# Writes of padding rows spread between the row loads of an expert layer

## What is computed

```python
x = _layernorm(x + attention(x))
scores = softmax(xf @ gate_w.T)                    # 4096 tokens, 8 experts
top_vals, top_idx = top_k(scores, 2)
h = einsum('td,ehd->teh', xf, W1)                  # only for the chosen experts
y, g = split(h, 2); eo = einsum('teh,edh->ted', y * silu(g), W2)
z = einsum('te,ted->td', w_dense, eo)
z = z + _gated_mlp(xf, Ws1, Ws2)                   # the shared expert, all tokens
x = _layernorm(x + z)
```

## Time and profile before

| | |
|---|---|
| median of 3 runs | 350.71 us (349.76 to 352.3) |
| the profiled execution | 349.76 us |
| its span | 348.0 us |
| TensorE busy | 313.3 us, 90% of the span |
| VectorE busy | 265.5 us, 76% |
| GpSimd busy | 195.8 us, 56% |
| ScalarE busy | 192.8 us, 55% |
| mean granted TensorE clock | 0.966 |

### The profile page before, as it was taken

How to read it: one execution, slowest core, us unless ns; L and a number is a source line. 1 busy time by engine, 2 the same in 40 slices (tenths; PEclk the granted TensorE clock), 3 DMA queues, 4 the chain that set the end, 5 groups by cost and what they waited for, 6 DMA issues and landing times.

```text
span 348.0 us, 7780 instructions
## 1 busy us (share of the span) xinstructions
PE 313.3 (90%) x2225; PEld 281.1 (81%) x2225; DVE 265.5 (76%) x1037; ACT 192.8 (55%) x425; POOL 195.8 (56%) x223
## 2 busy tenths in 40 slices
PE   2889899999999989999998999999999999999800
PEld 1456688689788878888898999999999999999700
DVE  1796679766889898975577776676668998988786
ACT  1053787545565454635234566655565558868863
POOL 4049641746687858785372444444757685677620
PEclk9989999899999999999999999999999999999955
DMA  7968320311381202262145344444899798899668
GB/s 218 382 232 273 121 63 0 110 35 63 107 206 50 94 33 94 82 189 78 65 168 148 120 129 132 131 129 126 183 252 196 191 242 194 209 238 261 186 211 337
DMA packets 31383, 54.63 MB, mean 157 GB/s; under 512 B 4880, under 2 KB 22544, under 8 KB 31344
## 3 DMA queue, kind: packets, MB, share of 16 engines
q1 hardware_dynamic: 23136, 29.82, 28.8%
q0 software_dynamic: 8208, 24.32, 24.8%
HBM read 29.73 MB, written 24.40 MB: 156 GB/s over the span
## 4 chain that ended last, share of the span: by engine, by line
PE 63%; DVE 14%; DMA 8%; POOL 6%; ACT 4%; issue 3%; SPq 2%; POOLq 0%; DVEq 0%; ACTq 0%
PE bank L1061 21%; PE bank L945 12%; PE bank L1087 11%; PE bank L1070 5%; PE bank L1030 4%; PE bank L967 4%; DMA stage<-ws_t 4%; PE bank L930 3%; DVE xs L1173 3%; DVE htlo L1378 2%; POOL rows_in L559 2%; DVE mix L1373 2%; POOL w1lo L515 2%; DMA rows_out<-stage,place 1%; DMA stage<-w_t 1%
## 5 line engine op out<-in xcount | busy, mean ns | idle before, releaser
L599 POOL DMA_INDIRECT rows_out<-stage,place x71 | 69.2, 974 | 60.5 <-ACT stage L768 45.0
L559 POOL DMA_INDIRECT rows_in<-x,slot x64 | 65.2, 1019 | 50.2 <-DVE slot L1288 33.6
L1061 PE MATMUL bank<-w1hi,xthi 128*128 x142 | 39.2, 357 | 1.1 <-DVE xs L1384 1.1
L748 ACT ACTIVATE stage<-bank 128x384 f32<-128x384 f32 (+1 forms) x36 | 17.5, 487 | 40.5 <-PE bank L1061 40.5
L768 ACT ACTIVATE stage<-bank,weight 128x256 f32<-128x256 f32 x71 | 30.0, 471 | 15.5 <-PE bank L1087 15.4
L1061 PE MATMUL bank<-w1lo,xthi 128*128 x142 | 36.2, 336 | 0.0
L1061 PE MATMUL bank<-w1hi,xtlo 128*128 x142 | 36.2, 335 | 0.0
L686 ACT ACTIVATE mix<-bank 128x512 f32<-128x512 f32 x24 | 14.2, 592 | 36.3 <-PE bank L945 36.3
L1390 DVE TENSOR_TENSOR xtlo<-bank,xthi 128x512 fp32r<-128x512 f32 (+1 forms) x36 | 24.3, 676 | 11.1 <-ACT xthi L694 10.8
L1518 DVE TENSOR_TENSOR stage<-bank,stage 128x384 f32<-128x384 f32 (+1 forms) x36 | 19.8, 550 | 15.7 <-ACT stage L748 15.5
L945 PE MATMUL bank<-xthi,ws1hi 128*128 128x512 f32 x96 | 31.8, 412 | 0.0
(11 more groups left out here) (242 smaller groups left out, 895.6 us busy)
## 6 DMA issues: line engine op xcount, KB each, us to landing
stage<-rows_in SPq DMA_DIRECT2D x71, 133.0 KB, 2.9
xs<-rows_out POOLq DMA_DIRECT2D x12, 512.0 KB, 6.7
xs<-x SPq DMA_DIRECT2D x8, 512.0 KB, 8.7
out<-xs SPq DMA_DIRECT2D x7, 512.0 KB, 5.1
stage<-w_t SPq DMA_DIRECT2D x8, 384.0 KB, 3.9
rows_in<-clear SPq DMA_DIRECT2D x16, 133.0 KB
rows_out<-stage,place POOLq DMA_INDIRECT x71, 3.5
stage<-w_t SPq DMA_DIRECT2D x2, 512.0 KB, 3.9
```

What stands on the lines that cost most here:

```text
L559: pool.indirect_dma_start(rows_in[0:E * CAP, :], bass.IndirectOffsetOnAxis(slot[:, q * G + t, k:k + 1], 0), x2[q % 2][:, t, :], None).then ...
L599: pool.indirect_dma_start(rows_out[:, :], bass.IndirectOffsetOnAxis(place[:, 2 * j + b:2 * j + b + 1], 0), by[j % 4][:, b * C:(b + 1) * C] ...
L748: act.activation(bsg[j % 2][:, 0:width(j)], bank_h[j % 2][:, 0:width(j), H:F], ACT.Silu).then_inc(s_bsg, 1)
L1061: mm = pe.matmul(bank_h[j % 2][:, b, 0:F], bx[j % 2][:, (2 * b + k) * P:(2 * b + k + 1) * P], w[:, bass.ds(e, 1), k, :], start=(a == 0), s ...
```

## The change

Before, SyncE issues all 8 writes of padding in a row and then loads pairs 4 to 7. Now it loads pair 4, then issues 2 writes, loads pair 5, issues 2 writes, and so on to pair 7. The wait for `zrow` stays in front of pair 4. What is transferred, and all waits, are the same; only SyncE's program is reordered.

```diff
             for j in range(4):
                 load_rows(j)
             sp.wait_ge(s_ends, 1)
-            for e in range(E):
-                r = sp.value_load(zrow[0:1, e:e + 1], min_val=0, max_val=ROWS - P)
-                sp.dma_start(rows_in[bass.ds(r, P), :], clear[:]).then_inc(s_pad, 16)
+            share_of = E // (FULL // 2 - 4)
             for j in range(4, FULL // 2):
                 load_rows(j)
+                for e in range((j - 4) * share_of, (j - 3) * share_of):
+                    r = sp.value_load(zrow[0:1, e:e + 1], min_val=0, max_val=ROWS - P)
+                    sp.dma_start(rows_in[bass.ds(r, P), :], clear[:]).then_inc(s_pad, 16)
             for n in range(2):
                 sp.wait_ge(s_sc[n], 16 * K * G * NP)
             sp.wait_ge(s_pad, 16 * (IDLE + E))
```

## The result

| | median | range | runs |
|---|---|---|---|
| before | 351.07 us | 349.17 to 353.08 | 20 |
| changed | 354.1 us | 350.81 to 356.33 | 20 |

The ratio is 1.0072, with a 95% interval of 1.0049 to 1.0093: the changed kernel is slower, by about 2.5 us, or 3.0 us by the medians. I had forecast no change and a range up to 353.0. So the loss is under 1%, but it is real, and the median lies outside the range.

What follows compares the result with a forecast made beforehand. TensorE was taken to bound the kernel, busy 313.3 of 348.0 us. Pair 4, pairs 5 to 7, pair 8 and contention each added 0, so 349.76 us stayed, 350.7 as a median; range 349.2 to 353.0.

Steps and rivals of the forecast that it cites:

- The transposes of pair 5 began at 199.86: TensorE's transposes (L1030): pair 5's start read as 199.86 us, pairs 6 and 7 following in rounds of 4.12 us.
- the transposes of pair 8, which began at 212.22: TensorE's start on pair 8's rows, read as 212.22 us; the latest time by which pair 8's loads must land.
- The rival on the hand-over: Change-over to expert blocks: without writes beside last scatters or first loads, experts start up to 0.99 us earlier, 349.7; chance 0.04.
- The slack of 2.2 us: Pair 8: its second load was to land at 210.0 us, 2.2 us ahead of its transposes at 212.22.
- pair 8 comes late: Waiting for padding delays pair 8 if landings exceed 7.9 us; chance 0.08 for 1 to 3 us, 0.03 for over 3.5.
- the sign of being wrong that I had named: Idle time ahead of L1030 at about 212 us, ended by a row load, or a clock below 1.00 behind it.
- the writes did not hold up pair 4 before: SyncE at pair 4: its load waited for VectorE's places (184.31 us), not the writes; moving them brings nothing.
- SyncE's step of 1.12 us: SyncE's queue: each load or write in the run of pairs 4 to 7 takes 1.12 us to issue.
- the order of the run of 16: SyncE from 185.12 us: load, load, write, write, four times, the last write issued at 201.9 us.
- pair 8 as the tight place: SyncE's wait for all padding ahead of pair 8: first load at 205.6 us instead of 200.64; forecast cost 0.
- The slack of pairs 5 to 7: Row loads of pairs 5, 6 and 7 land 6.2, 5.8 and 5.4 us ahead of their transposes; delays cost nothing.
- So a short stall should cost itself only: TensorE's clock: it stayed 1.00 after about a microsecond idle ahead of 184.25 us, so no extra cost from a stall.

Runs made afterwards that it cites:

- r9: Changed kernel plus eight SyncE register loads from zrow ahead of pair 4, values unused, no writes from them; median 363.99 us, ratio 0.9996 to the kernel before.
- r11: Changed kernel plus three more writes behind pair 7 into a DRAM tensor nothing reads, waited for only at the end; 362.25 us, ratio 0.9941 to the kernel before.
- r6: The changed kernel measured again, no edit; median 361.65 us, ratio 0.9942 to the kernel before in the same group.
- r5: The kernel before measured and profiled again, no edit; median 363.66 us, ratio 1.0006 to the kernel before in the same group.
- r10: Changed kernel plus eight more writes ahead of pair 4, to fixed rows nothing reads, without register loads; 364.88 us, ratio 1.0019 to the kernel before.
- r15: Changed kernel with two writes ahead of pair 4, two behind each of pairs 4 to 6, none behind pair 7; 361.35 us, ratio 0.9905 to the kernel before.
- r1: The changed kernel measured again, no edit; median 361.98 us, ratio 0.9952 to the kernel before in the same group.

## Why the prediction was wrong

**The step that failed** is "The transposes of pair 5 began at 199.86", and with it "the transposes of pair 8, which began at 212.22". I took the first product at 184.25 us for that of pair 0. It is pair 1's. The timeline of the kernel before has L1061 already here, right behind the last shared products, and that is pair 0:

```profile
180.34 0.28 PE L967 MATMUL bank<-ws2lo,hthi 128*128 128x256 f32 x1
180.46 0.52 PE L1061 MATMUL bank<-w1hi,xthi 128*128 x2
```

All rounds are one pair further than I counted. The rows headed "pair 5 and pair 8" are of pairs 6 and 9, and pair 8's transposes began at 208.10. (The rival on the hand-over has the same slip: the transposes at 195.90 are pair 5's.) The slack of 2.2 us was really 2.2 - 4.12 = -1.9, and the measured idle time is 2.06. With the right round the same sum gives a loss of 1.9 us. The same holds for the rival "pair 8 comes late", to which I gave 0.08 and 0.03: it begins where the two landings together exceed 7.9 - 4.12 = 3.8 us, not 7.9, and they took 3.02 + 2.97. The idle time had been in my own numbers, and the sign of being wrong that I had named, an idle time ahead of L1030 with a low clock behind it, is what came, one round earlier.

**What held:** the writes did not hold up pair 4 before, SyncE's step of 1.12 us, the order of the run of 16, and pair 8 as the tight place: loads from 205.83 against 205.6. The slack of pairs 5 to 7 was smaller by 4.12 us too (2.1, 1.7 and 1.3 us), and still enough; no idle time shows there.

**The sizes:** for the landing of the last write I took 2.7 us from the scatters; it was 3.02, and the 2.3 us that the prediction sets beside it were further off. I had 210.0 for the second load; it was 210.24.

**The clock.** "So a short stall should cost itself only" was wrong in this execution: the 2.06 us were followed by a product of 3.65 in place of 2.09 us. The term was left out of the sum for a stall; with it the loss is 3.6 us, about what the medians show (3.0). I can't say in how many executions it fell. The four fastest of the 20 changed runs (350.81 to 351.35) took about as long as the kernel before, so there not even the idle time shows in the end; the others lie between 352.5 and 356.3. The one trace, with its span of 354.0, is not of one of these four.

**The rival "the hand-over gets faster"**, at 0.04, was wrong in the first measurement and right in the four groups of the experiments. What r9 shows to be enough for it there, SyncE's register instructions beside those of the other engines, I hadn't thought of; I had only weighed transfers. The change-over is also where the sign of this change turns: 0.7% slower where the change-over idles 1.1 us, 0.5 to 0.6% faster where it idles 5.

**What stays open:** why the kernel before takes 364 us in the experiments and 351 in the first measurement. Its two traces (spans 348.0 and 361.2) show only where: 1.9 us ahead of pair 0's first product, 6.1 from there to pair 8's transposes, about 4.5 from pair 9's to TensorE's last product, and 0.7 behind it. It also stays open whether the loss of 0.7% there is pair 8 and the clock and nothing else: the trace shows both on the path, but the kernels that take them away were not run under those conditions.

## What to carry to other kernels

When a slack is read from a periodic trace, anchor the count at both ends: find the first item of the period by its number of instructions and the last one too, before a slack smaller than one period is believed. When work is moved behind others on a queue that ends in a wait for landing, the last item pays its landing in full: put the last write at least its own landing, the steps of the load and the landing of the load ahead of the first reader. Two writes ahead and none behind pair 7 does that; it was the fastest order at 364 us and is untried at 351. And count the instructions of an issue, not only its transfer; beside a dense stretch of other engines these had a price of their own (r9).

## What the runs showed of the hardware

- Eight register loads of SyncE, with nothing issued from them, raised TensorE's idle time at the change-over from 0.9 + 1.9 us (r11) to 5.05 (r9), and VectorE's from 1.1 (r6) to 4.0, though the loads had ended 3 us before TensorE's idle time began. In the kernel before under these conditions (r5), with such loads and writes behind them, single register instructions took up to 0.71 us in place of 0.03 to 0.15.
- The low clock did not go by the length of the idle time: 2.06 us were followed by a clock of 0.50 (first trace of the changed kernel), 3.67 us in r10 and 2.9 us in r15 were not, 5.2 us in r5 were. 0.94 + 1.94 us in r1 were followed by 0.50, 0.89 + 1.94 us at the same place in r11 were not.
